# Layer 0 attention: query/key projections and their splitting moved to earlier units, in halves; the gate moved behind the variance, with two silu buffers

## The reference, cut to what matters

```python
xn = _layernorm(x)
s = _L0_attn_ref(xn, ...)            # differential attention: two softmax maps, att1 - lam * att2
g = _silu(_L0_ffn_ref(xn, ...))      # 8 experts, the best 2 of each token
x = x + s * g
xn = _layernorm(x)
s = _L1_attn_ref(xn, ...)            # attention over a window of 128 tokens
g = _silu(_L1_ffn_ref(xn, ...))
return x + s * g
```

## Time and profile before

| what | value |
|---|---|
| times of three runs | 1350.69, 1353.15, 1356.68 us, median 1353.15 us |
| profiled execution | span 1353.5 us from the first to the last instruction |
| busy share of the span | PE 79%, DVE 60%, ACT 59%, POOL 45% |
| attention of layer 0 | about 231 to 768 us |
| attention of layer 1 | about 979 to 1349 us |
| full steps of layer 0 | 28.5 us each, the last ones about 25 us |
| full steps of layer 1 | about 20.5 us each |

### The profile page before, as it was taken

One profiled execution on the slowest core, in us unless ns is written; L12 is line 12 of the kernel. 1 busy time (PEld: TensorE's weight loads), 2 busy tenths in 40 slices (PEclk: granted clock), 3 DMA queues, 4 the chain that ended last, 5 costly groups with the idle time before them and its releaser, 6 DMA issues. The chain is left out here.

```text
span 1353.5 us, 38128 instructions
## 1 busy us (share of the span) xinstructions
PE 1071.2 (79%) x12376; PEld 808.5 (60%) x12376; DVE 809.8 (60%) x1668; ACT 799.8 (59%) x1892; POOL 615.5 (45%) x918
## 2 busy tenths in 40 slices
PE   4359998588999798899987344999857888978885
PEld 3349998355565455556554244999824655655553
DVE  4676664568777577777751357666436664755641
ACT  4845555057777677777776342655514665656663
POOL 6256553023455456555665416655303242444443
PEclk9999999579999899999998555999958898989997
DMA  6402222322332222232200340222212122222210
GB/s 181 113 24 69 70 69 47 93 56 58 85 77 58 58 57 65 67 85 68 57 20 9 94 109 16 71 69 68 55 47 63 44 64 66 55 62 64 52 48 20
DMA packets 144615, 86.43 MB, mean 64 GB/s; under 512 B 16547, under 2 KB 138037, under 8 KB 144469
## 3 DMA queue, kind: packets, MB, share of 16 engines
q1 hardware_dynamic: 135828, 66.72, 18.9%
q0 software_dynamic: 8640, 17.71, 5.6%
HBM read 30.06 MB, written 15.60 MB: 34 GB/s over the span
## 5 line engine op out<-in xcount | busy, mean ns | idle before, releaser
L1424 DVE TENSOR_REDUCE at_maxima<-ps 128x2 f32<-128x512 f32 (+1 forms) x576 | 371.7, 683 | 226.3 <-PE ps L1117 223.9
L1313 ACT ACTIVATE at_probs<-ps 128x512 f32<-128x512 f32 x576 | 320.8, 598 | 108.8 <-PE ps L1117 104.2
L1116 PE MATMUL ps<-tables 64*128 64x256 bf16 (+1 forms) x2304 | 229.6, 260 | 128.9 <-DMA stack<-at_pieces 62.3
L1117 PE MATMUL ps<-stack 62*128 62x256 bf16 (+3 forms) x3072 | 265.6, 255 | 2.4 <-issue 2.4
L717 ACT ACTIVATE ex_hid<-ps,ex_w 128x128 f32<-128x128 f32 x568 | 162.0, 368 | 120.3 <-PE ps L690 111.2
L1116 PEld LDWEIGHTS ps<-tables 64*128 64x128 bf16 x2304 | 91.7, 96 | 229.7 <-issue 193.9
L646 POOL DMA_INDIRECT ex_rows<-xn_rows,ex_ids_now x142 | 143.7, 1012 | 110.4 <-PE ps L681 68.7
L1117 PEld LDWEIGHTS ps<-stack 62*128 62x128 bf16 (+1 forms) x3072 | 167.1, 99 | 13.7 <-issue 2.6
L750 DVE COPY ex_w<-weights 128x1156 f32 x142 | 109.3, 769 | 103.8 <-issue 102.8
L1005 POOL DMA_INDIRECT at_chosen_y<-list_out,at_slot x128 | 130.1, 1017 | 55.3 <-issue 29.0
L690 PE MATMUL ps<-ex_rowsT,ex_w 128*128 128x128 f32 x1136 | 154.8, 281 | 0.0
(11 more groups left out here) (188 smaller groups left out, 1504.2 us busy)
## 6 DMA issues: line engine op xcount, KB each, us to landing
stack<-at_pieces SPq DMA_DIRECT2D x192, 128.0 KB, 2.7
stack<-at_pieces SPq DMA_DIRECT2D x192, 64.0 KB
list_out<-ex_result SPq DMA_DIRECT2D x142, 64.0 KB, 1.5
weights<-in_L_w SPq DMA_DIRECT2D x4, 1024.0 KB, 5.6
weights<-in_L_w SPq DMA_DIRECT2D x16, 256.0 KB, 6.6
xn_rows<-xn SPq DMA_DIRECT2D x8, 512.0 KB, 3.3
ex_rows<-xn_rows,ex_ids_now POOLq DMA_INDIRECT x142, 2.6
x<-in_L_attn_x SPq DMA_DIRECT2D x4, 512.0 KB, 6.1
```

The source lines that it names most:

```text
L1116: return nc.tensor.matmul(fine(bank, j), R.eye[tile, j, :], mask[tile], start=(j == 0), stop=True, skip_group_check=(j > 0))
L1117: return nc.tensor.matmul(bank[:, j - 2, :], left(j - 2)[tile], right(j - 2)[tile], start=False, stop=True, skip_group_check=True)
L1313: nc.scalar.activation(probs[:, (n // 3) % 2, n % 3, i * 512:(i + 1) * 512], t_bank[i], ACT.Exp, scale=SCALE).then_inc(t_free, 1)
L1424: nc.vector.tensor_reduce(by_half[:, h0:h0 + heads, a], s_bank[i].rearrange("p (m k) -> p m k", k=P * (late + 1)), AX.X, ALU.max).then_inc ...
```

## The change

In layer 0 five uses get other units: `qk0` and `qk1` go from units 6 and 7 to 4 and 5, `out` from unit 1 to 7, `v` from unit 5 to 11, so that `out` now follows `qk1`. The split is done for `qk0` (half 0) and `qk1` (half 1) apart, in six instructions of half the width: half 0 in units 5, 6, 7 and half 1 in units 8, 9, 10, where the three full-width ones were in 8, 9, 10. `split` waits for its own half's bank alone. Layer 1 uses the same function, so there too each of the three instructions becomes two, in the same two units as before.

On POOL layer 0's `gate` moves from the head of the step to behind `head_variance`, ahead of `fetch_ffn`. Since `mix_ffn` and the silu of a batch now come ahead of the gate of the batch before it, `silu` has two buffers, and `mix_ffn` waits for the last silu to be finished, since `ffn` is overwritten. To make room, the normalised tokens `xn` are kept only until the experts are done.

```diff
-        ORDER = (("rows", 0), ("out", 1), ("turn10", 2), ("turn11", 3), ("v", 5), ("qk0", 6), ("qk1", 7),
-                 ("shift", 8), ("turn00", 9), ("turn01", 10))
+        ORDER = (("rows", 0), ("turn10", 2), ("turn11", 3), ("qk0", 4), ("qk1", 5), ("out", 7), ("shift", 8),
+                 ("turn00", 9), ("turn01", 10), ("v", 11))
...
-        SPLIT = {8: (0,), 9: (1,), 10: (2,)}
+        SPLIT = {5: ((0, 0),), 6: ((0, 1),), 7: ((0, 2),), 8: ((1, 0),), 9: ((1, 1),), 10: ((1, 2),)}
...
-        SPLIT = {3: (0, 1), 5: (2,)}
+        SPLIT = {3: ((0, 0), (1, 0), (0, 1), (1, 1)), 5: ((0, 2), (1, 2))}
...
             def mix_ffn(b):
                 lone_wait(pool, gathered, (b + 1) * (16 * QB * TOPK))
+                lone_wait(pool, silu_ready, b)
...
-            def gate(step, b):
+            def gate(step, b, p):
+                silu = silu_of[p]
...
-                if has(step, "out"):
-                    gate(step, step - 2)
+                if layer and has(step, "out"):
+                    gate(step, step - 2, r % 2)
                 if has(step, "last"):
                     mix_ffn(step - 1)
                     if layer == 0:
                         head_variance(step - 1)
+                if layer == 0 and has(step, "out"):
+                    gate(step, step - 2, r % 2)
                 if has(step, "now"):
                     fetch_ffn(step)
...
-            def split(step, r, b, part):
+            def split(step, r, b, half, part):
                 pieces = pieces_of[(r + SPLIT_AHEAD) % 2]
+                of = slice(half * A, half * A + A)
                 if part == 0:
-                    dve.wait_ge(g_free, use(step + SPLIT_AHEAD - 3, "qk1") + 1)
-                    nc.vector.tensor_tensor(whole[:], whole[:], pieces[:, 0], ALU.subtract).then_inc(split_chain, 1)
+                    dve.wait_ge(g_free, use(step + SPLIT_AHEAD - 3, f"qk{half}") + 1)
+                    nc.vector.tensor_tensor(whole[:, of], whole[:, of], pieces[:, 0, of], ALU.subtract).then_inc(split_chain, 1)
```

More of the change, by code:

```diff
@@ L862, in build_attention @@
         ffn = sb("ffn", [P, QB, C])
-        silu = sb("silu", [P, QB, C])
+        silu_of = [sb(f"silu{p}", [P, QB, C]) for p in range(2)]
         if layer == 0:
@@ L1325, in log_stat, with sigmoid_ffn @@
                 nc.scalar.activation(rstd[:], rstd[:], ACT.Exp, scale=-0.5).then_inc(rstd_ready, 1)
-            def sigmoid_ffn(b):
+            def sigmoid_ffn(b, p):
+                silu = silu_of[p]
                 act.wait_ge(ffn_ready, b + 1)
@@ L1392, in body @@
                     if has(step, "last") and n == SILU - 1:
-                        sigmoid_ffn(step - 1)
+                        sigmoid_ffn(step - 1, 1 - r % 2)
                     for name in NAMES:
@@ L1400, in _ @@
         def _(dve):
-            def split(step, r, b, part):
+            def split(step, r, b, half, part):
                 pieces = pieces_of[(r + SPLIT_AHEAD) % 2]
+                of = slice(half * A, half * A + A)
                 if part == 0:
-                    dve.wait_ge(g_free, use(step + SPLIT_AHEAD - 3, "qk1") + 1)
-                    nc.vector.tensor_tensor(whole[:], whole[:], pieces[:, 0], ALU.subtract).then_inc(split_chain, 1)
+                    dve.wait_ge(g_free, use(step + SPLIT_AHEAD - 3, f"qk{half}") + 1)
+                    nc.vector.tensor_tensor(whole[:, of], whole[:, of], pieces[:, 0, of], ALU.subtract).then_inc(split_chain, 1)
                 elif part == 1:
-                    dve.wait_ge(split_chain, b * 2 + 1)
-                    nc.vector.tensor_copy(pieces[:, 1], whole[:]).then_inc(split_chain, 1)
-                else:
-                    dve.wait_ge(split_chain, b * 2 + 2)
-                    nc.vector.tensor_tensor(pieces[:, 2], whole[:], pieces[:, 1], ALU.subtract).then_inc(pieces_ready, 1)
+                    dve.wait_ge(split_chain, b * 4 + 2 * half + 1)
+                    nc.vector.tensor_copy(pieces[:, 1, of], whole[:, of]).then_inc(split_chain, 1)
+                else:
+                    dve.wait_ge(split_chain, b * 4 + 2 * half + 2)
+                    nc.vector.tensor_tensor(pieces[:, 2, of], whole[:, of], pieces[:, 1, of], ALU.subtract).then_inc(pieces_ready, 1)
             def search(b, n):
@@ L1446, in split_shift, with gate_values @@
                 nc.vector.tensor_tensor(shift_p[:, 1, :], shift_t[:], shift_p[:, 0, :], ALU.subtract).then_inc(shift_p_ready, 1)
-            def gate_values(b):
+            def gate_values(b, p):
+                silu = silu_of[p]
                 dve.wait_ge(silu_exp, b + 1)
@@ L1494, in body @@
                     if has(step, "last") and n == SILU:
-                        gate_values(step - 1)
+                        gate_values(step - 1, 1 - r % 2)
                     if has(step, "shift") and n == SLOT["shift"]:
@@ L1503, in body @@
                     if has(step, "split"):
-                        for part in SPLIT.get(n, ()):
-                            split(step, r, step + SPLIT_AHEAD, part)
+                        for half, part in SPLIT.get(n, ()):
+                            split(step, r, step + SPLIT_AHEAD, half, part)
             schedule(dve, body)
@@ L1559, in build @@
                 R.weights = until_experts.enter_context(nc.sbuf_tensor(f"weights{layer}", [P, EXPERTS, WIDTH], F32))
+                R.xn = until_experts.enter_context(nc.sbuf_tensor(f"xn{layer}", [P, NT, C], F32))
                 if layer == 0:
```

5 lines of the change are left out of this document (2 added, 3 removed).

## The result

The changed kernel takes **1376.4 us** (median of four runs, 1374.9 to 1379.2) against 1353.5 us for the kernel before beside it: a ratio of 1.016, interval 1.014 to 1.0186. It is slower by 23 us, outside the predicted range.

| stretch | before | after | difference | predicted |
|---|---|---|---|---|
| first projection to first `rows` | 107.8 | 101.0 | -6.7 | -5.5 (-7 to -3) |
| eleven full steps | 319.9 | 340.1 | +20.2 | +4.4 (0 to 11.6) |
| four last steps of layer 0 | 93.4 | 96.2 | +2.8 | +1 (0 to 2) |
| from there to the end, layer 1 in it | 599.2 | 602.1 | +2.9 | +2.4 (0 to 7) |

The account below looks back on a forecast made before the run. PE was taken as nearly the bound, with a loop through POOL's gate to set the new step. 1353.5 - 5.5 (start) + 4.4 (full steps) + 1 (drain) + 2.4 (layer 1) = 1355.8, say 1356 us; range 1344 to 1373.

Parts of the forecast that it names:

- The loop: Layer 0: `rows`, units 1 to 7, `out`, gate, fetch, normalisation, next `rows`; 28.9 us a step, +4.4 us over eleven steps.
- the second rival: DVE blocks POOL more, at the second half's subtraction and the division's product: loop 30.0 us, 1369 us; chance 0.18.
- PE's wait in unit 7: Layer 0, unit 7: PE's scores wait for the bank that ACT's exponential frees, a new wait of about 1.5 us.
- PE's wait at `rows`: Layer 0, start of a step: PE waits for POOL's L995, 28.9 - 26.1 - 1.5 = 1.3 us.
- the clock rival: PE's clock falls to half behind its new wait at `rows`: +22.5 us on the full steps, 1374 us; chance 0.12.
- the term of the full steps: Eleven full steps of layer 0, each 0.4 us longer by the loop: +4.4 us, bounds 0 and 11.6.
- The clock's price: Half of 3.3 us lost in each of eleven layer 0 steps if the clock fell: 11 x 1.65 us.
- The start: First steps of layer 0, where no `rows` is due: splitting in halves gains 5.5 us, bounds -7 and -3.
- The step of 26.1 us: Layer 0's full step if only PE's own work counted: 28.5 - 2.4 = 26.1 us.
- The drain: Last steps of layer 0: the gate's 1.69 us goes in front of the normalisation, +1 us, bounds 0 and 2.
- Layer 1: Half-width instructions cost 0.15 us for all three pairs, 16 times: +2.4 us, bounds 0 and 7.

Follow-up runs that it names:

- e1: Changed kernel with layer 0's gate and its wait for `out` moved behind the normalisation: 1338.0 us, 0.988 of before.
- e12: Changed kernel with `out` back in unit 1 and layer 0's gate back at the head of POOL's step, the rest kept: 1340.4 us, 0.988 of before.
- e2: Changed kernel with 8 useless transposes added on PE in layer 0, ahead of its wait for the rows: 1361.3 us, 1.005 of before.
- e3: Changed kernel with `out` back in unit 1, the gate still behind the variance: 1356.1 us.
- e4: Changed kernel with layer 0's copy of the slots moved from behind the gate to ahead of it: 1351.4 us, 0.9975 of before.
- e5: Changed kernel with layer 0's silu in unit 3 instead of unit 5 (DVE's part in unit 4): 1357.7 us.
- e7: e1 with layer 0's split again in three whole-width instructions in units 8, 9 and 10: 1347.0 us.
- e6: e1 with layer 0's silu also moved to unit 3: 1325.7 us, 0.979 of before.
- e9: e1 with the same 8 transposes as in e2 added ahead of `rows`: 1342.8 us, 0.993 of before.

## Why the prediction was wrong, point by point

- **The loop** was found, and its mechanism holds: `e1` and `e12` open it in two ways and both take 36 to 38 us off. At full clock it is 29.35 us (`e2`) against 28.9 taken and 28.5 to 29.55 as bounds. The mis-sized part is the stretch from the slots to L995: I let L995's 1 us of blocking go by half, and it went wholly, but came back at the slots' copy (1.05 for 0.19 us) and in smaller pieces behind it. This is the place that the second rival named. By "SBUF — State Buffer" ("Who interferes with whom") of the Trainium skill a GpSimd instruction that reads SBUF is kept out while DVE reads two SBUF inputs. The trace agrees, with the copy ending at 603.95 and DVE's second subtraction at 603.90. DVE's side of it shows too (0.81 us for the first half's subtraction and 0.95 us for the silu product during the variance, instead of 0.67 and 0.41); as forecast, PE's wait in unit 7 stays ACT's 1.5 us.
- **PE's wait at `rows`** is the step of the prediction that failed. I put it at 28.9 - 26.1 - 1.5 = 1.3 us and held against the clock rival that waits of 0.9 us had left the clock alone. The wait is 2.1 us: the loop is 0.45 us longer, and PE's own part is shorter than the 26.1 that I had from subtracting waits from one step (`e2`: 29.35 less 1.10 of wait, 1.5 for ACT and 1.09 added is 25.7; in the trace before, the step from 518.23 to 546.61 us gives 25.7 as well). Two errors of under half a microsecond each add up in the difference on which the clock hangs, and the clock then costs 10.7 us where the sum had nothing for it. Of the 15.8 us by which the term of the full steps is off, these are 10.7 and the loop's length 5.0.
- **The clock's price**, 11 x 1.65 = 18 us in the rival, is 10.7 us by `e2`: it falls in most full steps, not in all, and a step with it is about 1.2 us longer. That the rival's 1374 us came near the measured time is luck: its clock was 7 us too dear and its loop 5 us too short. That PE's clock goes to half after idling is what the Trainium skill says ("TensorE: Matmul & The Clock Gate", "What's actually happening"). The traces agree that it falls behind a wait, but not behind every one: outside the long step all waits of up to 1.5 us at `rows` in the full steps (`e2`, `e3`, `e4`) left it at 1.00, and between 1.7 and 2.4 us some were followed by the lower clock and some weren't, the longer ones not more surely (`e5`).
- **The start** was right (-6.7 for -5.5; `e7` shows about 3.5 of it to be the halves), and so were ACT's 1.5 us in unit 7 (with the silu earlier, `e5` and `e6`, a step is about a microsecond shorter: 28.0 for 29.3 us at full clock, and 26.5 for 27.5). The step of 26.1 us that was to come "if nothing else came up" was not reached; the nearest is `e6`, 26.5 us with PE busy 25.7.
- **The drain** was +2.8 for +1, outside its bounds; at three of its `rows` PE waits 2 to 2.8 us there too.
- **Layer 1** can't be judged: +2.4 forecast, +2.9 read off with what lies around it, and the same code scatters over 9 us between traces.
- **No term at all** stood for the gain in the steps that the loop hid. With the loop undone (`e12`) the rest of the change is worth 12 us in the full steps and 16 us in all against the kernel before run beside it (1356.9 us).

## What to carry to other kernels

When an instruction that waits for a late result is put ahead of work that the next step's first use needs, follow the whole loop through every engine, and then look at what the engine at its end does while it waits: here half the loss was the loop and half PE's clock behind a 2 us wait. A forecast that rests on a small difference of two long sums (29.4 - 27.2) should give the other outcome a real chance. Adding useless work at the wait is a cheap test of it: here it helped where the standstill itself cost something (`e2`) and cost 5 us where there was none (`e9`); the cure is to take the wait off the loop (1338 us), and then what comes next (1326 us).

## What was not expected of the hardware

- 1.09 us of useless transposes per step made the kernel 15 us faster (1376.4 to 1361.3 us), and moving a copy of 128x4 values, which takes 0.19 us alone, made it 25 us faster.
- A wait of 2.43 us was followed by a clock of 1.00 and others of 1.84 and 2.13 us by the lower level, and of two of 2.14 us in one trace only the second: the length alone doesn't decide. What else does is open.
